# Peak products of the 64-wide cross attention: four of a key block at once, in pairs on the two halves of the array

## The reference, cut to what matters

```python
x = layer_norm(context, ln_m_g, ln_m_b)          # (2, 4096, 256)
lat = layer_norm(latents, ln_l_g, ln_l_b)        # (2, 256, 256)
q = lat @ Wq                                     # 16 heads of 64
k, v = jnp.split(jnp.concatenate([x, lat], axis=1) @ Wkv, 2, axis=-1)   # 4352 keys
dots = jnp.einsum('bhid,bhjd->bhij', q, k) * scale
out = jnp.einsum('bhij,bhjd->bhid', jax.nn.softmax(dots, axis=-1), v)
return out.reshape(b, m, heads * dim_head) @ Wout
```

## Time and profile before

| | |
|---|---|
| median of 3 runs | 3938.63 us (3932.94 to 3941.34) |
| the profiled execution | 3929.64 us, span from first to last instruction 3927.8 us |
| granted TensorE clock, mean over the span | 0.921 |
| busy in the span | PE 84%, weight loads 52%, DVE 58%, ACT 38%, POOL 23% |
| this stage | from about 640 to 1860 us of the span, in 8 groups |

### The profile page before, as it was taken

The page is one execution under the profiler, slowest core; times in us unless marked ns, Lnnn a source line. Parts: engine busy times, 40 slices in busy tenths (PEclk is TensorE's granted clock), DMA queues, the critical chain, the costliest instruction groups (busy, mean ns, idle before and its releaser), DMA issues. The chain is left out here.

```text
span 3927.8 us, 54884 instructions
## 1 busy us (share of the span) xinstructions
PE 3305.8 (84%) x20909; PEld 2024.7 (52%) x20968; DVE 2274.1 (58%) x3668; ACT 1509.9 (38%) x2233; POOL 903.5 (23%) x666
## 2 busy tenths in 40 slices
PE   6968796999999999999579396999775689994659
PEld 4835494665665656656336374444443444442225
DVE  4325314665664665655478205999562389974954
ACT  2315211433333334334256131677551146772311
POOL 1023001425425335345147012000020300000520
PEclk9969898999999999999789698999887899997879
DMA  4238552000001000000486416666003366620011
GB/s 173 102 127 272 207 219 81 6 6 4 7 1 55 9 4 7 6 1 1 133 297 233 173 44 168 128 126 131 14 19 114 88 162 127 132 50 22 0 41 43
DMA packets 228564, 346.74 MB, mean 88 GB/s; under 512 B 104016, under 2 KB 177424, under 8 KB 223696
## 3 DMA queue, kind: packets, MB, share of 16 engines
q1 hardware_dynamic: 227920, 342.16, 29.6%
q0 software_dynamic: 384, 1.05, 0.1%
HBM read 257.15 MB, written 86.02 MB: 87 GB/s over the span
## 5 line engine op out<-in xcount | busy, mean ns | idle before, releaser
L1539 DVE TENSOR_REDUCE L1x_pk<-L1x_psm 128x1 f32<-128x512 f32 (+1 forms) x576 | 374.9, 661 | 179.8 <-PE L1x_psm L1368 169.9
L1338 POOL TENSOR_TENSOR L1x_acc<-L1x_acc,L1x_pr 128x512 f32<-128x512 f32 x256 | 416.3, 1626 | 137.4 <-ACT L1x_pr L1515 119.0
L1515 ACT ACTIVATE L1x_pr<-L1x_pss 128x1024 f32<-128x1024 f32 x272 | 278.6, 1024 | 288.0 <-PE L1x_pss L1427 280.5
L1561 DVE TENSOR_TENSOR L1x_acc<-L1x_acc,L1x_pr 128x512 f32<-128x512 f32 x256 | 261.3, 1021 | 201.9 <-ACT L1x_pr L1515 197.5
L1148 DVE TENSOR_REDUCE L3x_pk<-L3x_psm 128x1 f32<-128x512 f32 x512 | 328.2, 685 | 35.2 <-PE L3x_psm L985 31.4
L1148 DVE TENSOR_REDUCE L2x_pk<-L2x_psm 128x1 f32<-128x512 f32 x512 | 328.3, 685 | 34.5 <-PE L2x_psm L985 30.6
L1125 ACT ACTIVATE L3x_pr<-L3x_pss 128x1024 f32<-128x1024 f32 x256 | 248.1, 1021 | 103.7 <-PE L3x_pss L1026 103.4
L1125 ACT ACTIVATE L2x_pr<-L2x_pss 128x1024 f32<-128x1024 f32 x256 | 248.1, 1021 | 101.8 <-PE L2x_pss L1026 101.5
L1388 PE MATMUL L1x_pss<-L1x_cT,L1x_w 128*128 128x512 f32 (+1 forms) x576 | 277.0, 571 | 3.6 <-DMA L1x_cT<-normed_context 2.7
L1427 PE MATMUL L1x_pss<-L1x_Q,L1x_K 64*128 64x256 f32 x2176 | 279.3, 376 | 0.0
L1393 PE MATMUL L1x_pss<-L1x_w,L1x_cT 128*128 128x256 f32 x1088 | 278.4, 380 | 0.8
(11 more groups left out here) (661 smaller groups left out, 5775.2 us busy)
## 6 DMA issues: line engine op xcount, KB each, us to landing
f0e_wt<-in_f_pieces SPq DMA_DIRECT2D x10, 3072.0 KB, 11.2
offset_rows<-s_rows SPq DMA_DIRECT2D x32, 768.0 KB, 5.3
L2x_KS<-L2x_key_parts SPq DMA_DIRECT2D x24, 1024.0 KB, 13.0
L3x_KS<-L3x_key_parts SPq DMA_DIRECT2D x24, 1024.0 KB, 13.1
s_add<-offset_rows SPq DMA_DIRECT2D x32, 512.0 KB, 6.6
n_cT<-in_ctxT SPq DMA_DIRECT2D x32, 512.0 KB, 4.7
f1e_wt<-in_f_pieces SPq DMA_DIRECT2D x8, 2048.0 KB, 15.0
L2x_key_parts<-n_kst SPq DMA_DIRECT2D x32, 384.0 KB, 2.8
```

The lines of the kernel that those rows point to most:

```text
L1338: i = nc.gpsimd.tensor_tensor(acc[:, n, 1, :, :], acc[:, n, 1, :, :], pr[:, A % RING, :, 1, :], ALU.add)
L1515: nc.scalar.activation(pr[:, A % RING, :, :, :].rearrange("p h e q -> p (h e q)"), pss[:, x:x + 2, :].rearrange("p h n -> p (h n)"), ACT.E ...
L1539: nc.vector.reduce_max(pk[:, m, hq, j:j + 1], psm[:, i % 2, 0:NQ[j][1]], AX).then_inc(peak_read, 1)
L1561: i = nc.vector.tensor_tensor(acc[:, n, 0, :, :], acc[:, n, 0, :, :], pr[:, A % RING, :, 0, :], ALU.add)
```

## The change

The four peak products of a key block (two heads, two query halves) become one step of the loop: `PEAKS` falls from 72 to 18 a group. Head h contracts its own 64 partitions only, so `qzb` with its zeros and half copies gives way to `Qb`, a plain bf16 copy of the queries (one DVE copy for a chunk instead of two), and the two heads' products stand next to each other on the two halves of the array's rows, in two banks. Query half 0 goes to both banks of `psm`, half 1 to banks 2 and 3 of `pss`. DVE reads each pair by one reduction over two banks with two results. Step i waits for both reductions of step i - 1, and step 0 for the last group's `o_done` and exponentials. Key and value tiles alternate between banks 0 and 1 of `pss` (`n % 2`), and tile n waits for the eviction of tile n - 2. Score step 1 also waits for all reductions.

A step now falls at the end of a tile (`more` is 0 or 1, and `done + (c + 1) * more // 2` puts one after the second half).

```diff
@@ -1244,9 +1244,8 @@
     TILES = NK + NV
     STEPS = KT // 2
     ALL = KC * STEPS
-    PART = NB * 4
-    PEAKS = KC * PART
-    QEV = 3 * KC
+    PEAKS = KC * NB
+    QEV = 2 * KC
 
     names = ("c_load0 c_load1 c_load2 c_load3 latents nt_here wq_load wk_load wv_load q_mm q_ev tile_mm tile_ev k_cast peaks peak_read peak rows row_in "
              "scored exps averaged sum_dve sum_pool den o_done chain").split()
@@ -1255,16 +1254,12 @@
         V = t.sb(pre + "_V", [P, KT, 4, hd])
         K = t.sb(pre + "_K", [P, KC, KEYS])
         Kb = t.sb(pre + "_Kb", [P, KC, KEYS], BF16)
-        qzb = t.sb(pre + "_qzb", [P, 2, KC, 2, S], BF16)
+        Qb = t.sb(pre + "_Qb", [P, 2, KC, S], BF16)
         mrow = t.sb(pre + "_mrow", [P, KC, 2, S], BF16)
         with stage(nc, pre + "_fill", pre + "_fill1") as (block, _u, _v):
             @block.gpsimd
             def _(pool):
                 nc.gpsimd.memset(mrow[:, :, :, :], 0.0)
-
-            @block.vector
-            def _(dve):
-                nc.vector.memset(qzb[:, :, :, :, :], 0.0)
 
         with nc.Fori(0, B) as b:
             with Tensors(nc) as u, stage(nc, *[pre + "_" + n for n in names]) as (block, *sems):
@@ -1275,7 +1270,7 @@
                 w = u.sb(pre + "_w", [P, 3, KC, D])
                 nt = u.sb(pre + "_nt", [P, KC, S])
                 Q = u.sb(pre + "_Q", [P, 2, KC, S])
-                pk = u.sb(pre + "_pk", [P, KC, 4, NB])
+                pk = u.sb(pre + "_pk", [P, KC, QT, 2, NB])
                 mx = u.sb(pre + "_mx", [P, KC, 4])
                 acc = u.sb(pre + "_acc", [P, 2, 2, 2, S])
                 pr = u.sb(pre + "_pr", [P, RING, 2, 2, S])
@@ -1292,12 +1287,10 @@
 
                     if t_ < 2:
                         return 0
-                    return min(PEAKS, 4 * (t_ - 1), -(-PEAKS * (t_ - 1) // (TILES - 2)))
-
-                def peak_of(i):
-                    m, rest = divmod(i, PART)
-                    j, hq = divmod(rest, 4)
-                    return m, j, hq
+                    return min(PEAKS, -(-PEAKS * (t_ - 1) // (TILES - 2)))
+
+                def peak_banks(qt):
+                    return psm[:, :, :] if qt == 0 else pss[:, 2:4, :]
 
                 @block.sync
                 def _(sp):
@@ -1345,7 +1338,7 @@
                         if g == 0:
                             pe.wait_ge(nt_here, 1)
                         else:
-                            pe.wait_ge(peak_read, PEAKS * g)
+                            pe.wait_ge(peak_read, QT * PEAKS * g)
                         for m in range(KC):
                             for c in range(KC):
                                 i = nc.tensor.matmul(psm[:, 0, m * S:(m + 1) * S], w[:, 0, c, m * P:(m + 1) * P], nt[:, c, :],
@@ -1354,27 +1347,30 @@
 
                     def peak_products(g, first, last):
                         for i in range(first, last):
-                            m, j, hq = peak_of(i)
-                            h, qt = divmod(hq, 2)
+                            m, j = divmod(i, NB)
                             o, w_ = NQ[j]
                             if i == 0:
                                 pe.wait_ge(q_ev, QEV * (g + 1))
-                            if hq == 0:
-                                pe.wait_ge(k_cast, NK * g + m * NB + j + 1)
-                            if i == 1 and g >= 1:
-                                pe.wait_ge(o_done, KC * g)
-                            if i >= 2:
-                                pe.wait_ge(peak_read, PEAKS * g + i - 1)
-                            nc.tensor.matmul(psm[:, i % 2, 0:w_], qzb[:, g % 2, m, h, qt * P:(qt + 1) * P], Kb[:, m, o:o + w_],
-                                             start=True, stop=True).then_inc(peaks, 1)
+                                if g >= 1:
+                                    pe.wait_ge(o_done, KC * g)
+                                    pe.wait_ge(exps, ALL * g)
+                            pe.wait_ge(k_cast, NK * g + i + 1)
+                            if i >= 1:
+                                pe.wait_ge(peak_read, QT * (PEAKS * g + i))
+                            for qt in range(QT):
+                                for h in range(2):
+                                    half = slice(64 * h, 64 * h + 64)
+                                    p = nc.tensor.matmul(peak_banks(qt)[:, h, 0:w_], Qb[half, g % 2, m, qt * P:(qt + 1) * P], Kb[half, m, o:o + w_],
+                                                         start=True, stop=True)
+                                p.then_inc(peaks, 1)
 
                     def tile(g, n):
-                        x, done = n % 4, peaks_by(n - 1)
+                        x, done = n % 2, peaks_by(n - 1)
                         more = peaks_by(n) - done
-                        if n >= 4:
-                            pe.wait_ge(tile_ev, TILES * g + n - 3)
+                        if n >= 2:
+                            pe.wait_ge(tile_ev, TILES * g + n - 1)
                         elif g >= 1:
-                            pe.wait_ge(exps, ALL * g - (n < 2))
+                            pe.wait_ge(exps, ALL * g - 1)
                         if n == 0:
                             pe.wait_ge(wk_load, 16 * (g + 1))
                         if g == 0 and n < NB:
@@ -1403,7 +1399,7 @@
                             pe.wait_ge(row_in, 2 * U) if m else pe.wait_ge(o_done, U)
                         for h in range(2):
                             for qt in range(QT):
-                                i = nc.tensor.matmul(pst[64 * h:64 * h + 1, qt * P:(qt + 1) * P], mx[:, m, 2 * h + qt:2 * h + qt + 1],
+                                i = nc.tensor.matmul(pst[64 * h:64 * h + 1, qt * P:(qt + 1) * P], mx[:, m, 2 * qt + h:2 * qt + h + 1],
                                                      k.ident[:, :], start=True, stop=True)
                         i.then_inc(rows, 1)
 
@@ -1413,6 +1409,8 @@
                             pe.wait_ge(tile_ev, TILES * (g + 1))
                         if s == 0:
                             pe.wait_ge(row_in, 2 * (KC * g + n + 1))
+                        if a == 1:
+                            pe.wait_ge(peak_read, QT * PEAKS * (g + 1))
                         if a >= 2:
                             pe.wait_ge(exps, ALL * g + a - 1)
                         x = 2 * (a % 2)
@@ -1434,7 +1432,7 @@
                         pe.wait_ge(exps, A + 1)
                         if s == 0:
                             if n == 1:
-                                pe.wait_ge(peak_read, PEAKS * (g + 1))
+                                pe.wait_ge(peak_read, QT * PEAKS * (g + 1))
                             elif g >= 1:
                                 pe.wait_ge(o_done, U - 1)
                         out = averages_of(n)
@@ -1495,10 +1493,10 @@
                         if n < NK:
                             m, j = divmod(n, NB)
                             o, w_ = NQ[j]
-                            i = nc.scalar.copy(K[:, m, o:o + w_], pss[:, n % 4, 0:w_])
+                            i = nc.scalar.copy(K[:, m, o:o + w_], pss[:, n % 2, 0:w_])
                         else:
                             r = n - NK
-                            i = nc.scalar.copy(V[:, 2 * r:2 * r + 2, :, :].rearrange("p t h e -> p (t h e)"), pss[:, n % 4, :])
+                            i = nc.scalar.copy(V[:, 2 * r:2 * r + 2, :, :].rearrange("p t h e -> p (t h e)"), pss[:, n % 2, :])
                         i.then_inc(tile_ev, 1)
 
                     for g in range(GROUPS):
@@ -1528,18 +1526,18 @@
                         dve.wait_ge(q_mm, g + 1)
                         for m in range(KC):
                             nc.vector.tensor_copy(Q[:, g % 2, m, :], psm[:, 0, m * S:(m + 1) * S]).then_inc(q_ev, 1)
-                            for h in range(2):
-                                half = slice(64 * h, 64 * h + 64)
-                                nc.vector.tensor_copy(qzb[half, g % 2, m, h, :], psm[half, 0, m * S:(m + 1) * S]).then_inc(q_ev, 1)
+                            nc.vector.tensor_copy(Qb[:, g % 2, m, :], psm[:, 0, m * S:(m + 1) * S]).then_inc(q_ev, 1)
 
                     def read_peaks(g, first, last):
                         for i in range(first, last):
-                            m, j, hq = peak_of(i)
-                            dve.wait_ge(peaks, PEAKS * g + i + 1)
-                            nc.vector.reduce_max(pk[:, m, hq, j:j + 1], psm[:, i % 2, 0:NQ[j][1]], AX).then_inc(peak_read, 1)
-                            if i % PART == PART - 1:
-                                dve.wait_ge(peak_read, PEAKS * g + i + 1)
-                                link(nc.vector.reduce_max(mx[:, m, :], pk[:, m, :, :], AX))
+                            m, j = divmod(i, NB)
+                            for qt in range(QT):
+                                n = QT * (PEAKS * g + i) + qt + 1
+                                dve.wait_ge(peaks, n)
```

(4 more changed lines are left out.)

## The result

| | before | after |
|---|---|---|
| median of 8 runs | 3936.11 us (3930.47 to 3941.34) | 3925.91 us (3920.61 to 3928.97) |
| ratio of the runs | | 0.9974, 95% interval 0.9964 to 0.9985 |
| profiled execution, span | 3929.64, 3927.8 us | 3928.29, 3926.5 us |

The kernel became 0.26% faster, 10 us of 3936; the forecast was 7.4. The two profiled executions lie only 1.3 us apart, because that of before was one of the fastest of its kind. So the totals of single traces say nothing at this size; the stretches inside them do, since those of the second and later groups of a batch repeat to 0.01 us.

A forecast was written before the change was run, and what follows sets the result against it. PE was taken to bound both stretches of a head group, with DVE following. Terms of -7.3, +5.1, +1.4, +0.2 and -0.3 gave -0.9 us a group, -7.4 over eight: 3931.2 us from the median, range 3916 to 3945.

The forecast's parts named there:

- pairs for single products: Peak products on PE: two half-height products issue together at the cost of one, 0.215 us; -7.3 us a group.
- switches: Array shape changes around each peak block: exposed load and drains, 0.305 us a block, 18 blocks; +5.1 us a group.
- neighbour waits: PE waits for DVE's reductions where blocks follow in adjacent tiles: three waits of 0.48 us; +1.4 us a group.
- wait for the last output: A group's first block waits for the last group's output: 0.67 us for 0.50, +0.2 in six of eight groups.
- narrow-tile wait of the old kernel: At the narrow key tile, an old wait for DVE goes: 0.74 us where two records need 0.43; -0.3 a group.
- part 3: Hand-over to DVE: a block waits for both earlier reductions, PE hears 0.05 us after they end; +1.4 us a group.
- Part 4: First block of a group: waiting for the last group's output adds 0.2 us, a narrow-tile wait of 0.3 goes.
- Two banks and DVE's copies: Tiles in two banks instead of four, and two query copies less per block of heads on DVE: costed at nothing.
- Rival A: Array shape switches nearly free, hidden behind pulled-ahead loads: -42 us, 3896 us; 5%, another 5% for something between, about 3915.
- B: Two-bank reductions cost more than their elements, DVE becomes the bound: slower, 3961 us at 1.7 us each, up to 4024; 6%.
- C: Paired peak products don't overlap because they read one operand tile: +7.3 us a group, 3989 us; 3%.
- D: The parts cancel exactly with a switch at 0.35 us: 3938 us, counted inside the forecast's 81%.

The follow-up runs named there:

- e1: New kernel with the pairs undone: peak products contract all 128 partitions with zero-padded queries, so the array never changes shape; 3942.42 us, ratio to old 1.001.
- e2: New kernel with each block's two pairs taken apart, one after either half of a tile, 17 more switches a group; 3971.91 us, ratio 1.0087.
- e7: Old kernel with key and value tiles in two banks instead of four, peak products as before; 3936.54 us, ratio 1.0008.
- e3: New kernel with DVE doing each block's first reduction twice, the extra result unread; 3961.03 us, ratio 1.0054.

## Why the prediction was right, and by which steps

The forecast case held: 7.4 us said, 10 measured, 6.6 of them in the stretches that the change touches. The number to compare with 7.4 is the 6.6. That they lie so close is partly luck: two terms were off by 0.3 each a group, in opposite directions. Its terms for a group with one before it, against what the traces show:

| term | forecast | measured |
|---|---|---|
| pairs for single products | -7.3 | -7.3 (pairs 0.21 apart; e1) |
| switches | +5.1 | +5.0 (14 x 0.30 and 4 x 0.2; e2 gives 0.30) |
| neighbour waits | +1.4 | +1.7 (0.57 each, not 0.48) |
| wait for the last output | +0.2 | -0.1 |
| narrow-tile wait of the old kernel | -0.3 | -0.3 |
| sum | -0.9 | -1.0; the stretch shows -0.87 |

- **Products and switches** came out as read from the pairs of the scores and from the same sequence in another stage. The rule of the Trainium skill (TensorEngine Tiling (Array Packing), Key Properties) that a change of mode drains the array is borne out here: a product of the other shape starts 0.31 to 0.32 us after the one before it instead of 0.215, and with the exposed load a round trip costs 0.30. The 2x of its table holds for the products themselves, 0.44 us for two in e1 and 0.21 for a pair here, and not for the stretch.
- **Neighbour waits** were undersized by 0.1 each. The term that was mis-sized is the hand-over from DVE to PE: 0.05 in part 3, read where one product of the old kernel waits, and 0.14 at a block (805.56 to 805.70). The change of shape is not the reason, for e1 has the same 0.14 without one. So a wait does swallow the drain, as the forecast had it. What makes the hand-over longer no run separates. In the code a later block stands behind two waits (the cast keys and the reductions), the old product behind one; that is a guess, not tested.
- **The wait for the last output** had the wrong sign. Part 4 set 0.67 against "0.30 and 0.20", brackets of the earlier trace rows. By starts the old kernel lost more: the first product came at 801.95 where 799.45 + 0.105 + 1.72 + 0.215 = 801.49 was due, 0.46, and the next at 802.54 for 802.16, 0.38. Now 0.72 stands where 0.84 stood. This and the former point cancel (-0.3 and +0.3 a group against the forecast).
- **The first group of a batch** should have gained 0.2 more than the others by part 4, and gained 0.2 less (0.65). There is no wait for an output in it, so the 0.12 saved on that wait (0.84 to 0.72) is missing, and so is the wait that hides a drain of 0.095.
- **Two banks and DVE's copies** cost nothing: e7, and the second stretch unchanged. No run tests the fill by itself; it ran once, for 0.91 us, beside POOL's of 0.95.
- **Rival A** (switches free) is refuted by e2, **B** by the 1.23 us of a reduction and by e3, **C** by the starts of the pairs. **D** lies close: by the forecast's own sum a switch at 0.35 would have given no change. The price of B counted two gaps over a narrow key tile in each group; e3 shows one, because the block before the second is narrow.

## What to carry to other kernels

Pairing half-height products beside full-height work pays only by what is left after the switches: here a block saved 0.43 us and paid 0.30, so the same change with one pair a block (0.215 saved) would lose. e2 is nearly that kernel, and it took 3972 us against 3938 for the old one. Price it from a place in the same trace where the two shapes already alternate. And where a hand-over goes from two banks in turn to all at once, spread the work by time and not by whole tiles: that was worth 17 us against the changed kernel (3909 for 3926), more than the change itself had brought. Whether the old kernel would gain from such spreading, at its own waits of 0.84 and 0.3 a group, was not tested.

## What the runs showed that I had not expected

- The idle time in a bracket understates what is lost at a wait, by 0.16 us for these products (0.41 for 0.57, 0.56 for 0.72), because the record before lasts beyond the start that its successor could have had.
- The hand-over from DVE to PE took 0.14 us from a block's reductions to the next block and 0.10 from the last output to the first block, against 0.05 at the single products of the old kernel; e1 shows that the array's shape has no part in it.
- All seven kernels with the new peak loop are 3.5 to 6.8 us faster than the sum of their stretches accounts for, and the cause is open.
- Stretches inside one stage repeat to 0.01 us between executions whose total times differ by 6 us (3929.64 and 3935.61 for the two of the old kernel).
